# Fused causal attention and MLP on one core: scores issued three steps ahead of context, totals summed three steps behind, nine evenly spread TensorE sums a group

## The chip, the cores and the metric

One core of a Trainium2 chip (trn2) runs the whole program. The metric is device time in microseconds, the median of several executions. TensorE, VectorE, ScalarE, GpSimd and the DMA queue of SyncE are written PE, DVE, ACT, POOL and SP in the rows of the profile; SP issues all the transfers named here.

## The reference

A transformer layer over 4096 tokens of width 512: attention with 16 heads of 32, layer norm of the residual, a SiLU-gated MLP with int32 weights and per-row scales, and a second layer norm. The change is in the attention:

```python
scores = jnp.einsum('bshd,bthd->bhst', q / jnp.sqrt(jnp.float32(HEAD_DIM)), k)
causal = jnp.triu(jnp.ones((S, S), dtype=bool), 1)
scores = jnp.where(causal, NEG_INF, scores)
attn = jax.nn.softmax(scores, axis=-1)
ctx = jnp.einsum('bhst,bthd->bshd', attn, v)
```

## The kernel before

Three stages follow one another: `project` (queries, keys and values, with their norms, to DRAM), `attend` (the stage that is changed) and `finish` (output projection, MLP, norms). `finish` begins when `attend` has ended on every engine.

`attend` works on four groups of four heads (`NG`, `HG`). In a group the 4096 queries are cut into eight chunks of 512, `ch` 0 to 7, and the keys into 32 blocks of 128, `kb`. A step is one chunk with one key block; chunk `ch` has 4(ch+1) steps, because only keys up to the chunk's end count, and a group has 144 steps (`NS`). In each chunk the four blocks on the diagonal come at places 0, 2, 4 and 6 with full blocks between them (in chunk 0 at places 0 to 3). A diagonal block is computed on 512, 384, 256 or 128 columns of queries (`cut`) and its first 128 columns are masked.

For each step:

- `scores` on TensorE: two units, `p` = 0 and 1, of two heads each. A unit writes one of three PSUM buffers (`RING` = 3), so unit u waits until ScalarE has read unit u-3.
- ScalarE: one exponential a unit, from PSUM into one of six `probs` buffers in SBUF (`PB` = 6). Step t waits until step t-6 has been read by both TensorE and VectorE (`valued`, `added`).
- GpSimd masks a diagonal block in place (line 826), once both exponentials are done.
- VectorE adds the step's probabilities to `total` (lines 1011 and 1016), for the softmax denominators. Place 0 of a chunk shares one add with place 1.
- `weigh` on TensorE (line 881): values times probabilities for four heads, added up in `ctx_acc` over the chunk. It waits for the exponentials, the mask, and at place 0 for `ctx_taken`.

In ten steps of a group (`by_pe`) TensorE does the adding instead: eight more matmuls with a matrix of ones into `sums_acc` (line 889), and VectorE skips the step. When a chunk is done, `sum_total` (TensorE, line 900) adds `total` over the partitions, VectorE copies the result out (`take_sums`, line 997), ScalarE copies the context out (`take_ctx`, line 936), and SP stores both.

TensorE runs in program order, one iteration a step: the scores of step t+2 (`LAG` = 2), then the context of step t, then `sum_total` of a chunk whose last step was t-2. At the end of a group `sum_total` of chunk 7 follows the last step directly.

SP's order matters in two places. In group 0 the loads of keys and values 2 to 7 stand ahead of the stores of chunk 0 and the queries of chunk 3. In every later group this is the order:

```python
load("q", 0); load("kv", 0); load("q", 1)
for j in range(1, NCH):
    load("kv", j)
store(sp, before, NCH - 1)     # waits for take_sums, chunk 7 of the group before
for ch in range(2, NCH):       # queries of chunk 2 first
    load("q", ch); store(sp, g, ch - 2)
```

Of the kernel before, what the change touches and what calls it, by code (L numbers as in the profile page):

```python
# [38 lines left out]
P = 128  # L39
# [539 lines left out]
def attend(nc, io, dr, keep):  # L579

    LAG = 2
    T_LAG = LAG + 2
    PB = 6
    RING = 3

# [24 lines left out]

    def by_pe(t):

        ch, kb = steps[t]
        return not diagonal(t) and t - first[ch] >= ST * 2 and (t - first[ch]) % 10 == 0
# [9 lines left out]
    def masks_before(t):  # L624
        return sum(diagonal(x) for x in range(t))

    with ExitStack() as c:
# [202 lines left out]
        def _(pe):  # L830
# [21 lines left out]
            def scores(g, t):  # L852
                ch, kb = steps[t]
                if t in first:
                    mine = q_chunks[q_buffer[ch]]
                    pe.wait_ge(q_in[q_buffer[ch]], 64 * len(mine) * g + 64 * (mine.index(ch) + 1))
                if kb == ST * ch:
                    pe.wait_ge(k_in[ch], 48 * g + 64)
                for p in range(2):
                    u = 2 * t + p  # L860

                    pe.wait_ge(exped, 2 * NS * g + u + 1)
                    for i in range(2):
                        h = 2 * p + i
                        ins = pe.matmul(score[u % RING][:, i, cut(t):], keys[0:ROWS, kb // ST, h, kb % ST * P:(kb % ST + 1) * P],  # L865
                                        queries[0:ROWS, q_buffer[ch], h, cut(t):], start=True, stop=True)
                    ins.then_inc(scored, 1)
# [47 lines left out]
            for t in range(LAG):  # L915
                scores(0, t)
            for g in range(NG):
                group(g, g < NG - 1)

        @block.scalar  # L920
        def _(act):
# [39 lines left out]
        def _(dve):  # L961
# [37 lines left out]
            for g in range(NG):  # L999
                for t in range(NS):  # L1000
                    ch, kb = steps[t]
                    place = t - first[ch]
                    if not by_pe(t) and (place or not ch):
                        dve.wait_ge(exped, 2 * NS * g + 2 * t + 2 + RING)
                        if diagonal(t) or place == 1:
# [3 lines left out]
                        if place > 1:  # L1009
                            dve.wait_ge(added, NA * g + adds_before(t) + A_CREDIT)  # L1010
                            dve.tensor_tensor(into, into, now, ALU.add).then_inc(added, 1)  # L1011
                        elif place == 1:
# [551 lines left out]
```

## Time and profile before

| what | value |
| --- | --- |
| median of 3 runs | 2407.95 us (2407.69 to 2412.66) |
| profiled execution | 2409.09 us, span of the trace 2407.3 us |
| attend, from first score matmul to last sum | 334.7 to 1557.6 us |
| busy over the whole span | TensorE 2328.8 us (97%), VectorE 1774.3, ScalarE 1315.9, GpSimd 271.7 |
| mean granted TensorE clock | 0.987 |

A row of a timeline gives start, duration, engine, line, operation and tiles, how many instructions were merged, and in brackets how long the engine was idle before and what released it. A context step and a PE sum are eight matmul records each; score steps are four. The ends of matmuls are modelled and overlap the next start a little, so the cost of an iteration is read from the start of its scores to the start of the next iteration's scores.

### The profile page before, as it was taken

Reading aid. Unit: us, or ns where it says so; the run is one execution under the profiler, and the core shown is the slowest. Engines: PE = TensorE matmul, PEld = TensorE weight load, DVE = VectorE, ACT = ScalarE, POOL = GpSimd, SP = SyncE. Lnnn points to the kernel's source line nnn. Section 1 sums busy time; section 2 is a strip of 40 time slices with the busy share of each in tenths; the row PEclk is TensorE's granted clock in tenths of the full one; section 3 lists DMA queues with packets and bytes.
Section 4 is the critical chain, followed back from the end, with each engine's and each line's share of the span. In section 5 each row is a group of like instructions: output and inputs, shape, how many; then the busy total and the mean of one; then the engine's idle time right before and its main releaser. Section 6 shows DMA issues by size and latency. Waiting matters only on the chain. (4 is left out here: it accounts for less than half of the span.)

```text
span 2407.3 us, 34361 instructions
## 1 busy us (share of the span) xinstructions
PE 2328.8 (97%) x12546; PEld 1403.8 (58%) x12546; DVE 1774.3 (74%) x1826; ACT 1315.9 (55%) x1631; POOL 271.7 (11%) x269
## 2 busy tenths in 40 slices
PE   8999979999999999999999999869999999999997
PEld 7888843333343333434334343358888888888885
DVE  7777748889888898888988889845556565565554
ACT  4444458888888888888888888711111111111111
POOL 2111112201122010221102111000000000000000
PEclk9999989999999999999999999979999999999998
DMA  7777794101811008110081100091111021110100
GB/s 250 255 247 248 233 246 94 39 7 24 166 41 36 19 10 180 41 32 23 6 181 45 32 23 6 20 312 35 36 36 53 19 70 35 36 53 18 35 18 18
DMA packets 126868, 197.42 MB, mean 82 GB/s; under 512 B 15064, under 2 KB 40152, under 8 KB 126688
## 3 DMA queue, kind: packets, MB, share of 16 engines
q1 hardware_dynamic: 126704, 195.25, 28.9%
q8 instruction: 101, 1.65, 0.3%
q14 instruction: 63, 0.52, 0.1%
HBM read 122.83 MB, written 72.37 MB: 81 GB/s over the span
## 5 line engine op out<-in xcount | busy, mean ns | idle before, releaser
L947 ACT ACTIVATE probs<-score 128x1024 f32<-128x1024 f32 (+3 forms) x1152 | 1024.8, 957 | 180.1 <-PE score L865 157.4
L1011 DVE TENSOR_TENSOR total<-total,probs 128x2048 f32<-128x2048 f32 (+3 forms) x472 | 982.4, 2081 | 77.9 <-POOL probs L826 35.3
L865 PEld LDWEIGHTS score<-queries,keys 98*128 98x128 f32 x2304 | 375.9, 189 | 495.9 <-ACT probs L947 409.4
L865 PE MATMUL score<-queries,keys 98*128 98x512 f32 (+3 forms) x2304 | 655.0, 406 | 6.4 <-ACTq L931 6.1
L881 PE MATMUL ctx_acc<-probs,values 128*32 128x512 f32 (+3 forms) x3584 | 441.3, 564 | 9.3 <-POOL probs L826 9.2
L1350 ACT ACTIVATE hidden<-slot,gate_scale_sb 128x512 f32<-128x512 f32 x128 | 88.0, 688 | 625.2 <-PE slot L1279 625.2
L826 POOL TENSOR_SCALAR_AFFINE_SELECT probs<-probs 128x512 f32<-128x512 f32 x128 | 193.2, 1510 | 1006.9 <-ACT probs L947 1006.9
L1435 DVE SCALAR_TENSOR_TENSOR hidden<-slot,up_scale_sb,hidden 128x512 f32<-128x512 f32 x128 | 96.1, 751 | 265.3 <-ACT hidden L1350 265.3
L1279 PE MATMUL slot<-xt_hi,wg_sb 128*128 128x512 f32 x512 | 201.8, 394 | 5.2 <-issue 5.2
L1279 PE MATMUL slot<-xt_lo,wg_sb 128*128 128x512 f32 x512 | 200.2, 391 | 3.2 <-issue 3.2
L1290 PE MATMUL y<-wd_sb,h_hi 128*128 128x512 f32 x512 | 199.4, 389 | 1.4 <-DVE h_lo L1443 1.4
L1279 PE MATMUL slot<-xt_hi,wu_sb 128*128 128x512 f32 x512 | 199.7, 390 | 0.0
L1279 PE MATMUL slot<-xt_lo,wu_sb 128*128 128x512 f32 x512 | 199.6, 390 | 0.0
L1290 PE MATMUL y<-wd_sb,h_lo 128*128 128x512 f32 x512 | 199.2, 389 | 0.0
L344 PE MATMUL acc<-w_hi,x_hi 128*128 128x512 f32 x384 | 163.9, 427 | 7.2 <-DVE w_lo L495 7.2
L881 PEld LDWEIGHTS ctx_acc<-probs,values 128*32 128x32 f32 x3584 | 71.7, 107 | 157.2 <-issue 127.2
L344 PE MATMUL acc<-w_hi,x_lo 128*128 128x512 f32 x384 | 151.1, 394 | 0.0
L344 PE MATMUL acc<-w_lo,x_hi 128*128 128x512 f32 x384 | 150.6, 392 | 0.0
L881 PE MATMUL ctx_acc<-probs,first_values 128*32 128x512 f32 (+3 forms) x1024 | 132.8, 591 | 0.0
L1221 POOL TENSOR_TENSOR rstd<-veps,minus_half 128x1 f32<-128x1 f32 x64 | 36.7, 573 | 807.0 <-DVE veps L1399 807.0
L1016 DVE TENSOR_TENSOR total<-probs 128x2048 f32<-128x2048 f32 (+1 forms) x32 | 71.2, 2226 | 58.1 <-ACT probs L947 57.0
L1279 PEld LDWEIGHTS slot<-xt_hi,wg_sb 128*128 128x128 f32 x512 | 96.6, 189 | 29.2 <-issue 9.1
(103 smaller groups left out, 2088.7 us busy)
## 6 DMA issues: line engine op xcount, KB each, us to landing
keys<-k_hi SPq DMA_DIRECT2D x64, 256.0 KB
queries<-q_hi SPq DMA_DIRECT2D x64, 256.0 KB
wq_int<-in_wq SPq DMA_DIRECT2D x48, 256.0 KB, 3.3
wq_float<-wq_f SPq DMA_DIRECT2D x48, 256.0 KB, 2.8
x_raw<-in_x_t SPq DMA_DIRECT2D x32, 256.0 KB, 3.8
v_rows<-v_out SPq DMA_DIRECT2D x32, 256.0 KB, 2.3
q_hi<-part_hi SPq DMA_DIRECT2D x32, 256.0 KB, 2.5
q_lo<-part_lo SPq DMA_DIRECT2D x32, 256.0 KB, 2.8
```

What stands on the lines that cost most here:

```text
L344: ins = pe.matmul(bank[:], x[:, par, dc, rows], w[:, dc, m * D:(m + 1) * D], start=dc == 0 and a == 0, stop=dc == DC - 1 and a == 2)
L826: pool.affine_select(out=view, in_=view, compare_op=ALU.is_ge, fill=0.0, base=0, pattern=[[0, HG], [1, P]], channel_multiplier=-1).then_in ...
L865: ins = pe.matmul(score[u % RING][:, i, cut(t):], keys[0:ROWS, kb // ST, h, kb % ST * P:(kb % ST + 1) * P], queries[0:ROWS, q_buffer[ch], ...
L881: ins = pe.matmul(ctx[h * HD:(h + 1) * HD, n0:], value(kb)[:, h * HD:(h + 1) * HD], probs[:, t % PB, h, n0:], start=t in first, stop=t in ...
L947: act.activation(probs[:, t % PB, 2 * p:2 * p + 2, cut(t):], score[u % RING][:, :, cut(t):], ACT.Exp).then_inc(exped, 1)
L1011: dve.tensor_tensor(into, into, now, ALU.add).then_inc(added, 1)
L1016: dve.tensor_tensor(into, probs[:, (t - 1) % PB, :, cut(t):], now, ALU.add).then_inc(added, 2)
L1221: pool.tensor_tensor(rstd[:, k, st:st + 1], veps[:, k, st:st + 1], minus_half[:], ALU.pow).then_inc(rooted[k], 1)
L1279: ins = pe.matmul(slot[pos % 2][q][:], v(w[:, i, dc * P:(dc + 1) * P]), v(x[:, par, dc, :]), start=dc == 0 and a == 0, stop=dc == DC - 1 a ...
L1290: ins = pe.matmul(y[st][:], v(x[:, i % 2, st * P:(st + 1) * P]), v(wd[:, i, :]), start=i == 0 and a == 0, stop=i == IC - 1 and a == 1)
L1350: act.activation(hidden[:, i % 2, :], slot[pos % 2][0][:], ACT.Silu, scale=gate_scale[:, i:i + 1]).then_inc(gated, 1)
L1435: dve.scalar_tensor_tensor(hid, slot[pos % 2][1][:], up_scale[:, i:i + 1], hid, ALU.mult, ALU.mult)\
```

## The change

TensorE's iteration t now issues the scores of step t+3, and `sum_total` follows three steps behind the end of a chunk. For chunk 7 this goes over the group's border: it is issued behind context step 2 of the next group, and `take_sums` behind step 3 of VectorE. The scores are counted in units, and ScalarE's `take_ctx` moves to the first unit of the third step of the next chunk. The steps that TensorE sums are nine a group, spread evenly over the full steps from place 8 on: steps 32, 50, 59, 76, 94, 103, 120, 130 and 139, in place of 22, 34, 50, 70, 80, 94, 104, 122, 132 and 142. No instruction of a transfer is added or moved in SP's order.

```diff
-    LAG = 2
-    T_LAG = LAG + 2
+    LAG = 3
+    TOTAL_LAG = 3
     PB = 6
     RING = 3
+    PE_SUMS = 9
...
+    late = [t for t in range(NS) if not diagonal(t) and place(t) >= 2 * ST]
+    pe_sums = {late[(2 * i + 1) * len(late) // (2 * PE_SUMS)] for i in range(PE_SUMS)}
+
     def by_pe(t):
 
-        ch, kb = steps[t]
-        return not diagonal(t) and t - first[ch] >= ST * 2 and (t - first[ch]) % 10 == 0
+        return t in pe_sums
...
+    scored_before = [2 * (t + LAG) + 2 for t in range(NS)]
+    taken_behind = {scored_before[last[ch]] - 2: ch for ch in range(NCH)}
...
-            def group(g, after):
-
+            def group(g, before, after):
+
+                done = early
                 for t in range(NS):
-                    if t + LAG < NS:
-                        scores(g, t + LAG)
-                    elif after:
-                        scores(g + 1, t + LAG - NS)
+                    for u in range(done, scored_before[t]):
+                        if u < 2 * NS:
+                            scores(g, u)
+                        elif after:
+                            scores(g + 1, u - 2 * NS)
+                    done = scored_before[t]
                     weigh(g, t)
-                    if t + LAG - T_LAG in last:
-                        sum_total(g, last.index(t + LAG - T_LAG))
-                sum_total(g, NCH - 1)
-
-            for t in range(LAG):
-                scores(0, t)
+                    if t - TOTAL_LAG in last:
+                        sum_total(g, last.index(t - TOTAL_LAG))
+                    elif before is not None and t == TOTAL_LAG - 1:
+                        sum_total(before, NCH - 1)
...
-                        if p == 0 and t - LAG in last:
-                            take_ctx(g, last.index(t - LAG))
-                        elif p == 0 and t == LAG - 1 and before is not None:
+                        if u in taken_behind:
+                            take_ctx(g, taken_behind[u])
+                        elif u + 2 * NS in taken_behind and before is not None:
                             take_ctx(before, NCH - 1)
...
-                    if t - T_LAG - 1 in last:
-                        take_sums(g, last.index(t - T_LAG - 1))
-                take_sums(g, NCH - 1)
+                    if t - TOTAL_LAG - 1 in last:
+                        take_sums(g, last.index(t - TOTAL_LAG - 1))
+                    elif g and t == TOTAL_LAG:
+                        take_sums(g - 1, NCH - 1)
+            take_sums(NG - 1, NCH - 1)
```

TensorE at the start of chunk 5 in group 0, before: the first row with 384 columns is the score of the chunk's place 2, and the row behind it the context of place 0.

```order
1978 L865 MATMUL score<-queries,keys 128x384 x4
1979 L881 MATMUL ctx_acc<-probs,values 32x512 x4
1980 L865 MATMUL score<-queries,keys 128x512 x4
1981 L881 MATMUL ctx_acc<-probs,first_values 32x512 x4
1982 L900 MATMUL sums_acc<-total,ones 32x512 x4
1983 L865 MATMUL score<-queries,keys 128x256 x4
1984 L881 MATMUL ctx_acc<-probs,values 32x384 x4
1985 L865 MATMUL score<-queries,keys 128x512 x4
1986 L881 MATMUL ctx_acc<-probs,first_values 32x512 x4
1987 L865 MATMUL score<-queries,keys 128x128 x4
1988 L881 MATMUL ctx_acc<-probs,values 32x256 x4
```

The same place after the change, from the score of place 2 on:

```order
1976 L874 MATMUL score<-queries,keys 128x384 x4
1977 L890 MATMUL ctx_acc<-probs,values 32x512 x4
1978 L898 MATMUL sums_acc<-probs,ones 32x512 x4
1979 L874 MATMUL score<-queries,keys 128x512 x4
1980 L890 MATMUL ctx_acc<-probs,values 32x512 x4
1981 L874 MATMUL score<-queries,keys 128x256 x4
1982 L890 MATMUL ctx_acc<-probs,first_values 32x512 x4
1983 L874 MATMUL score<-queries,keys 128x512 x4
1984 L890 MATMUL ctx_acc<-probs,values 32x384 x4
1985 L909 MATMUL sums_acc<-total,ones 32x512 x4
1986 L874 MATMUL score<-queries,keys 128x128 x4
```

Behind the score of place 2 there now stands the context of chunk 4's last step with a PE sum, and the context of place 0 comes only behind the score of place 3; each masked context step (512, 384 and 256 columns at places 0, 2 and 4) has one more score step ahead of it.

TensorE at the border of groups 0 and 1, before: `L900` is the total of chunk 7, and the scores of 384, 256 and 128 columns are steps 1, 2 and 3 of the new group.

```order
2154 L865 MATMUL score<-queries,keys 128x384 x4
2155 L881 MATMUL ctx_acc<-probs,values 32x512 x4
2156 L900 MATMUL sums_acc<-total,ones 32x512 x4
2157 L865 MATMUL score<-queries,keys 128x256 x4
2158 L881 MATMUL ctx_acc<-probs,first_values 32x512 x4
2159 L865 MATMUL score<-queries,keys 128x128 x4
2160 L881 MATMUL ctx_acc<-probs,first_values 32x384 x4
2161 L865 MATMUL score<-queries,keys 128x512 x4
2162 L881 MATMUL ctx_acc<-probs,first_values 32x256 x4
2163 L865 MATMUL score<-queries,keys 128x512 x4
```

The same place after the change:

```order
2154 L874 MATMUL score<-queries,keys 128x256 x4
2155 L890 MATMUL ctx_acc<-probs,values 32x512 x4
2156 L874 MATMUL score<-queries,keys 128x128 x4
2157 L890 MATMUL ctx_acc<-probs,first_values 32x512 x4
2158 L874 MATMUL score<-queries,keys 128x512 x4
2159 L890 MATMUL ctx_acc<-probs,first_values 32x384 x4
2160 L874 MATMUL score<-queries,keys 128x512 x4
2161 L890 MATMUL ctx_acc<-probs,first_values 32x256 x4
2162 L909 MATMUL sums_acc<-total,ones 32x512 x4
2163 L874 MATMUL score<-queries,keys 128x384 x4
```

The total of chunk 7 moved from directly behind the group's last context step to behind the context of step 2, past the scores of steps 3, 4 and 5 and three context steps. VectorE's copy of that sum (`sums_out<-sums_acc`) moved with it, from ahead of the adds of the new group to behind the first four of them:

```order
1625 L1034 COPY total<-probs 128x4x128
1626 L1030 TENSOR_TENSOR total<-probs 128x4x384
1627 L1025 TENSOR_TENSOR total<-total,probs 128x4x256
1628 L1025 TENSOR_TENSOR total<-total,probs 128x4x128
1629 L1012 COPY sums_out<-sums_acc 128x512
1630 L1030 TENSOR_TENSOR total<-probs 128x2048
```

## Rows read from the trace of the kernel before

**Rows 1.** Window of attend: busy PE, PEld, DVE, ACT, POOL; clock, DMA share, GB/s

```profile
334.70:1557.60 1222.90, 1212.87 (x7488) 486.42 (x7488) 1073.22 (x543) 1040.13 (x1184) 193.20 (x128) 1.00 0.25 54
```

**Rows 2.** Waits in attend: engine, line, released by: total us, times, longest

```profile
PE ctx_acc L881 <- POOL probs L826: 9.2, 28, 0.5
```

**Rows 3.** Timeline, steady steps of chunk 7, group 1

```profile
899.89 14.27 DVE L1011 TENSOR_TENSOR total<-total,probs 128x2048 f32<-128x2048 f32 x6
...
907.65 1.19 PE L865 MATMUL score<-queries,keys 98*128 98x512 f32 x4
908.50 1.94 ACT L947 ACTIVATE probs<-score 128x1024 f32<-128x1024 f32 x2 [0.18 <-PE score L865]
...
909.77 1.19 PE L865 MATMUL score<-queries,keys 98*128 98x512 f32 x4
```

**Rows 4.** Timeline, score steps around one PE sum

```profile
900.41 1.19 PE L865 MATMUL score<-queries,keys 98*128 98x512 f32 x4
...
903.39 1.20 PE L865 MATMUL score<-queries,keys 98*128 98x512 f32 x4
```

**Rows 5.** Timeline of TensorE, place 0 of chunk 4, group 1

```profile
726.87 0.97 PE L865 MATMUL score<-queries,keys 98*128 98x384 f32 x4
...
728.76 1.25 PE L865 MATMUL score<-queries,keys 98*128 98x512 f32 x4
```

**Rows 6.** Timeline, place 0 of chunk 5, group 1

```profile
767.53 2.29 DVE L1011 TENSOR_TENSOR total<-total,probs 128x2048 f32<-128x2048 f32 x1
767.60 2.71 POOL L826 TENSOR_SCALAR_AFFINE_SELECT probs<-probs 128x512 f32<-128x512 f32 x1 [29.66 <-ACT probs L947]
...
768.93 0.97 PE L865 MATMUL score<-queries,keys 98*128 98x384 f32 x4
769.07 0.60 ACT L936 ACTIVATE ctx_out<-ctx_acc 128x512 f32<-128x512 f32 x1 [0.39 <-PE ctx_acc L881]
...
770.42 1.06 PE L881 MATMUL ctx_acc<-probs,values 128*32 128x512 f32 x8 [0.52 <-POOL probs L826]
771.41 0.19 PEld L865 LDWEIGHTS score<-queries,keys 98*128 98x128 f32 x1 [0.84 <-ACT probs L947]
```

**Rows 7.** Timeline of TensorE, place 4 of chunk 4, group 1

```profile
735.37 0.66 PE L865 MATMUL score<-queries,keys 98*128 98x128 f32 x4
736.27 0.64 PE L881 MATMUL ctx_acc<-probs,values 128*32 128x256 f32 x8 [0.25 <-POOL probs L826]
736.84 0.50 PE L865 MATMUL score<-queries,keys 98*128 98x512 f32 x1
```

**Rows 8.** Timeline of TensorE, place 4 of chunk 2, group 1

```profile
677.03 0.66 PE L865 MATMUL score<-queries,keys 98*128 98x128 f32 x4
...
678.20 1.20 PE L865 MATMUL score<-queries,keys 98*128 98x512 f32 x4
```

**Rows 9.** The masks' line: least, median and most ns of one

```profile
L826 POOL TENSOR_SCALAR_AFFINE_SELECT probs<-probs x128: 630/1338/2736, 338.1 to 1499.5; 128x512 f32<-128x512 f32 x128
```

**Rows 10.** Timeline of TensorE, first score of chunk 3, group 0

```profile
382.19 1.06 PE L881 MATMUL ctx_acc<-probs,values 128*32 128x512 f32 x8
...
383.55 1.19 PE L865 MATMUL score<-queries,keys 98*128 98x512 f32 x4 [0.30 <-DMA queries<-shift]
```

**Rows 11.** Timeline of TensorE behind the border of groups 1 and 2

```profile
955.03 1.19 PE L865 MATMUL score<-queries,keys 98*128 98x512 f32 x4
...
968.91 1.19 PE L865 MATMUL score<-queries,keys 98*128 98x512 f32 x4
```

**Rows 12.** Timeline of SP there: stores of chunks 7 and 0

```profile
952.08 0.50 SPq L693 DMA_DIRECT2D sums<-sums_out  x1
...
968.05 0.50 SPq L693 DMA_DIRECT2D sums<-sums_out  x1
```

**Rows 13.** Windows there, columns as in the first group

```profile
961.00:963.00 2.00, 2.00 (x20) 0.69 (x12) 1.59 (x1) 1.35 (x3) 0.32 (x1) 1.00 0.07 18
...
975.00:977.00 2.00, 2.00 (x17) 0.95 (x17) 1.55 (x1) 1.74 (x3) 1.30 (x1) 1.00 0.01 3
```

More of the change, by code:

```diff
@@ L609, in diagonal, with place @@
         return steps[t][1] >= ST * steps[t][0]
+    def place(t):
+        return t - first[steps[t][0]]
+    late = [t for t in range(NS) if not diagonal(t) and place(t) >= 2 * ST]
+    pe_sums = {late[(2 * i + 1) * len(late) // (2 * PE_SUMS)] for i in range(PE_SUMS)}
     def by_pe(t):
-        ch, kb = steps[t]
-        return not diagonal(t) and t - first[ch] >= ST * 2 and (t - first[ch]) % 10 == 0
+        return t in pe_sums
     adds = [t for t in range(NS) if not by_pe(t)]
@@ L850, in _, with scores @@
             pe.sem_inc(totaled, 2)
-            def scores(g, t):
+            def scores(g, u):
+                t, p = divmod(u, 2)
                 ch, kb = steps[t]
-                if t in first:
+                if p == 0 and t in first:
                     mine = q_chunks[q_buffer[ch]]
                     pe.wait_ge(q_in[q_buffer[ch]], 64 * len(mine) * g + 64 * (mine.index(ch) + 1))
-                if kb == ST * ch:
+                if p == 0 and kb == ST * ch:
                     pe.wait_ge(k_in[ch], 48 * g + 64)
[L859 to L867, printed above, removed]
+                pe.wait_ge(exped, 2 * NS * g + u + 1)
+                for i in range(2):
+                    h = 2 * p + i
+                    ins = pe.matmul(score[u % RING][:, i, cut(t):], keys[0:ROWS, kb // ST, h, kb % ST * P:(kb % ST + 1) * P],
+                                    queries[0:ROWS, q_buffer[ch], h, cut(t):], start=True, stop=True)
+                ins.then_inc(scored, 1)
             def weigh(g, t):
@@ L901, in sum_total @@
                 ins.then_inc(totaled, 1)
-            def group(g, after):
+            def group(g, before, after):
+                done = early
                 for t in range(NS):
-                    if t + LAG < NS:
-                        scores(g, t + LAG)
-                    elif after:
-                        scores(g + 1, t + LAG - NS)
-                    weigh(g, t)
-                    if t + LAG - T_LAG in last:
-                        sum_total(g, last.index(t + LAG - T_LAG))
-                sum_total(g, NCH - 1)
-            for t in range(LAG):
-                scores(0, t)
+                    for u in range(done, scored_before[t]):
[4 more added lines that the diff above has]
+                    done = scored_before[t]
+                    weigh(g, t)
+                    if t - TOTAL_LAG in last:
+                        sum_total(g, last.index(t - TOTAL_LAG))
+                    elif before is not None and t == TOTAL_LAG - 1:
+                        sum_total(before, NCH - 1)
+            early = scored_before[NS - 1] - 2 * NS
+            for u in range(early):
+                scores(0, u)
             for g in range(NG):
-                group(g, g < NG - 1)
+                group(g, g - 1 if g else None, g < NG - 1)
+            sum_total(NG - 1, NCH - 1)
         @block.scalar
@@ L1001, in _ @@
                     ch, kb = steps[t]
-                    place = t - first[ch]
-                    if not by_pe(t) and (place or not ch):
+                    if not by_pe(t) and (place(t) or not ch):
                         dve.wait_ge(exped, 2 * NS * g + 2 * t + 2 + RING)
-                        if diagonal(t) or place == 1:
+                        if diagonal(t) or place(t) == 1:
                             dve.wait_ge(masked, NM * g + masks_before(t + 1))
```

4 lines of the change are left out of this document (2 added, 2 removed).

## The prediction

> **What bounds the kernel now.** I read the page's busy times first, then the window of attend alone, then the waits in it, then timelines. Attend takes 1222.9 us of the span, and TensorE is busy for 1212.9 of them at the full granted clock; VectorE is busy for 1073.2 and ScalarE for 1040.1 [rows 1]. So TensorE sets the stage's length with 10.0 us of gaps, and VectorE has 150 us to spare over the stage. The biggest gaps with a releaser are 28 waits of context steps for GpSimd's mask, 9.2 us in all, 0.5 the longest [rows 2]. A steady step shows why nothing else matters much: scores start at 907.65 and again at 909.77, 2.12 us a step, while ScalarE's two exponentials take 1.94 and then wait 0.18 for the next score [rows 3]. ScalarE runs right behind the scores. A long wait that the profile books on the exponentials for weight loads is no cost here, since the matmuls around it leave no gap.
>
> The depth of the look-ahead does not pace such a step. What ties scores to exponentials is the ring of three units, and that distance is the same with two or three steps ahead. What the look-ahead sets is how long an exponential and its mask have before TensorE wants them.
>
> **PE sums.** One iteration with a PE sum goes from 900.41 to 903.39, 2.98 us, against 2.12 without [rows 3, 4]: 0.86 us for a sum. One less in each of four groups gives 4 x 0.86 = 3.4 us. VectorE gets four more adds. Six adds in a row take 14.27 us, so 2.4 us each with its gap [rows 3]: 9.6 us more on an engine with 150 to spare. Locally it falls back 2.4 - 2.12 = 0.28 us a step until a PE sum or a chunk's place 0 lets it catch up. The last of those six adds starts at 899.89 + 14.27 - 2.29 = 911.87, while the exponentials of its step ended at 908.50 + 1.94 = 910.44: 1.4 us behind. A buffer is wanted again by the exponential six steps on, which starts five steps and a gap later, 5 x 2.12 + 0.18 = 10.8 us. An add that starts less than 10.8 - 2.3 = 8.5 us late costs nothing. One step that is no longer skipped adds 2.4, and the longest new stretch without a sum (chunk 5, 16 places) some 6 x 0.28 = 1.7 more. I cost the adds at nothing; the cover that hides them is this buffer slack.
>
> **Mask waits.** At place 0 of chunk 4, with no wait, an iteration takes 728.76 - 726.87 = 1.89 us [rows 5]; at place 0 of chunk 5 it takes 771.41 - 768.93 = 2.48 [rows 6]: 0.59 lost. At place 4 of chunk 4 it is 736.84 - 735.37 = 1.47, against 678.20 - 677.03 = 1.17 where nothing waits [rows 7, 8]: 0.30 lost. Of the 28 waits, 8 are of the first kind (chunks 2 and 5 of each group), 20 of the second. After the change each masked context step has one more score and context step ahead of it, at least some 1.2 us (the cheapest iteration, rows 8, is the bound from below), against at most 0.59 lost. So all should go, unless masks get later. Two of the 28, one of each kind, lie ahead of a load in group 0 and are taken out below. That leaves 7 x 0.59 + 19 x 0.30 = 9.8 us.
>
> How late can a mask be? The mask at place 0 of chunk 5 starts at 767.60, 0.07 us behind an add of 2.29 us, and takes 2.71 [rows 6]; the median is 1.34 and the most 2.74 [rows 9]. So it seems to stand still while the add runs. The Trainium skill (SBUF — State Buffer, SBUF: two separate sides) has a rule for that: a VectorE operation with two SBUF inputs and a GpSimd operation exclude one another for the whole instruction. By that rule more adds on VectorE mean more masks at the long end. If all masks took the 2.74 us of the longest, place 4's would come 2.74 - 1.34 = 1.4 us later than the median one, against the 1.2 to 2.1 us gained; I expect at most a few tenths to survive at some places, and the sum takes nothing for it.
>
> **Context taken.** At place 0 the context step also waits for ScalarE's copy of the last chunk's context, 769.07 to 769.67 in chunk 5 [rows 6]. Its place relative to the last context step is kept, and a full score step of 1.19 us instead of 0.97 now lies in between. No cost. The copy delays the exponentials behind it. The tightest spot that follows is the second score unit of place 4, which needs the first exponential of place 3: the copy ends 0.74 us after the next scores began (769.67 - 768.93), two exponentials of about 0.7 and 1.0 follow, so 2.4 us, and TensorE gets there after 2.12 + 0.35 = 2.5. Bounds: nothing, or up to 0.1 x 28 = 3 us. I take nothing, since the same race stands in the rows of before, one place earlier.
>
> **A load in group 0.** Chunk 3's first scores start at 383.55 on a DMA of queries [rows 10]. That load stands behind SP's loads of keys and values and does not hang on TensorE. TensorE would now reach these scores a context step sooner, and sooner by the waits removed before, and must wait for the same load. Everything won earlier in group 0 is lost there, and the context step that used to run ahead of this score, started at 382.19 and worth 1.06 us with a little overlap, now runs behind it: +1.0 us. The same holds for the longer fill at the start of attend, which costs nothing extra for that reason.
>
> **Queries of chunk 2 at the borders.** SP stores chunk 7's sum, then loads these queries. The store was issued at 952.08, and the transfers were nearly over in 961 to 963 [rows 12, 13]. The sum now comes after score step 5 and context step 2, which end in before at about 955.03 + 1.19 = 956.2; add 0.9 for VectorE's copy: the store goes out at 957.1, 5 us later. The next such store with its query load, issued at 968.05, has its traffic over in 975 to 977 [rows 12, 13], so 7 to 8 us from store to landing: 964.5 to 966 here. The scores of step 12 start at 968.91 [rows 11], after the change one context step and one mask wait sooner, 967.6. Slack 1.6 to 3 us where it was 6; no cost.
>
> **Tail.** After the last scores TensorE had two context steps, a PE sum and the last context step; now it has four context steps, much the same time, and the last add starts no later. 0.
>
> Sum: -3.4 - 9.8 + 1.0 = -12.2 us. The profiled execution would go from 2409.1 to 2396.9; it lies 1.1 above the median of the runs, 2407.95, so the median becomes 2395.75, and I say 2395.5.
>
> **Rivals.**
> - The mask waits only move: the next scores wait for their exponentials instead, and the gain is -3.4 + 1.0, or 2405.5 us. For it: ScalarE runs without a gap around places 1 to 3. Against it: it is idle 0.18 us in each steady step, and the price of the waits shows in start-to-start times. Chance 0.07.
> - VectorE falls six buffers behind in chunks 5 to 7: then each of its four extra adds comes onto the path, +9.6 in place of nothing, 2405 us. It needs adds 8.5 us late where I see 1.4 plus at most 4. Chance 0.03.
> - Slower: the queries of chunk 2 come late at three borders. Each us beyond the slack costs 3 us. It cancels the gain when they land 12.2 / 3 = 4.1 us beyond TensorE's arrival, so 6 to 7 us later than I reckon; at 6 us beyond, the time is 2395.5 + 18 = 2413.5. Nothing in the rows is that slow. Chance 0.03. A mild form, 1 to 2 us beyond, gives 2398.5 to 2401.5: chance 0.07.
> - My forecast: 0.80.
>
> **How the numbers follow.** A change of 0.2% is 4.8 us, about what this kernel's measurement can tell. Low end: small waits that I left out go too (attend's gaps are 10.0 us in all by modelled ends, but a wait of 0.25 by gap is 0.30 by starts, so up to 12 with the lesser ones), some 2 to 3 us more, and a run-to-run spread of 2: 2390.5. High end: the ring's 3 us and the mild load case: 2401. Faster is my case plus the mild load case, 0.87; same takes the first two rivals, 0.09; slower 0.04.
>
> **What would show it.** Right: no wait of context steps for masks; PE idle in attend near 3 us; the iteration at place 0 of chunk 5 without a gap; steady steps still 2.12; VectorE idle one or two us behind the fourth add of a group, waiting for the sum; the scores of chunk 3 in group 0 waiting about 2 us for queries. Wrong: a gap before the scores of step 12 in groups 1 to 3, ScalarE waiting for adds, or steady steps longer than 2.12.

## The result, and the profile after

| | median | runs | profiled |
| --- | --- | --- | --- |
| before | 2409.23 us | 4 (2407.69 to 2412.66) | 2409.09, span 2407.3 |
| after | 2391.01 us | 4 (2389.47 to 2391.17) | 2389.47, span 2387.7 |

The ratio is 0.9921, 95% interval 0.9904 to 0.9938. The change takes away 18.2 us by the medians and 19.6 by the two spans, where 12.2 were forecast. The direction held, and the size was half as much again as the sum said. The range, 2390.5 to 2401, was counted from a median of 2407.95 us. As a time, 2391.01 lies just inside it. But the ratio measured here, applied to 2407.95, gives 2388.9, and that is below the low end. One execution each of after_pad64, before_pad64 and six_placed in the experiments below took 3125 to 4510 us and is left out of their ratios.

I cut both spans at the first score matmul and at the end of attend's last sum. By spans the 19.6 us are 1.3 ahead of attend (334.7 to 333.4), 14.4 in attend (1222.8 to 1208.5) and 3.9 behind it (849.8 to 845.8).

The window of attend after, columns as in [rows 1]:

```profile
333.40:1541.90 1208.50, 1207.44 (x7456) 488.29 (x7456) 1094.79 (x547) 1038.86 (x1184) 166.16 (x128) 1.00 0.25 54
```

TensorE's gaps fell from 10.0 us to 1.1, and it does 32 matmuls less: four sums of eight. VectorE does four adds more, of 2.29 us, and is busy 21.6 us longer. Most of the rest are 41 adds that begin while a mask runs and take 2.5 to 2.8 us in place of 2.29, 10.7 us in all; before there was none such. The waits of attend's TensorE work after, columns as in [rows 2]:

```profile
PEld score L874 <- DMA queries<-shift: 0.8, 1, 0.8
...
PE ctx_acc L890 <- ACT ctx_out L951: 0.6, 3, 0.2
...
PE sums_acc L909 <- DVE total L1025: 0.4, 1, 0.4
```

The 28 waits for masks are gone. In their place stand three of 0.2 us for ScalarE's copy of the context, at the group borders. The start of chunk 5 in group 1, TensorE, VectorE, ScalarE and GpSimd, to be held against [rows 6]:

```profile
763.45 1.20 PE L874 MATMUL score<-queries,keys 98*128 98x512 f32 x4
764.58 1.07 PE L890 MATMUL ctx_acc<-probs,values 128*32 128x512 f32 x8
765.57 0.79 PE L874 MATMUL score<-queries,keys 98*128 98x256 f32 x4
766.29 1.07 PE L890 MATMUL ctx_acc<-probs,first_values 128*32 128x512 f32 x8
767.28 1.20 PE L874 MATMUL score<-queries,keys 98*128 98x512 f32 x4
...
752.16 7.08 DVE L1025 TENSOR_TENSOR total<-total,probs 128x2048 f32<-128x2048 f32 x3
761.45 2.29 DVE L1030 TENSOR_TENSOR total<-probs 128x2048 f32<-128x2048 f32 x1 [2.21 <-ACT probs L962]
...
763.59 0.60 ACT L951 ACTIVATE ctx_out<-ctx_acc 128x512 f32<-128x512 f32 x1 [1.34 <-PE sums_acc L898]
...
759.37 0.63 POOL L836 TENSOR_SCALAR_AFFINE_SELECT probs<-probs 128x512 f32<-128x512 f32 x1 [29.45 <-ACT probs L962]
```

The context of place 0 starts at 764.58; its mask had ended at 759.37 + 0.63 = 760.00, where before it ended 0.1 us ahead of the context step. The mask also takes 0.63 us in place of 2.71. It begins 0.13 us behind VectorE's last add (752.16 + 7.08 = 759.24), and VectorE then stands idle for 2.21 us, because one of the nine TensorE sums (step 59) is now chunk 4's last step. The iteration runs from 763.45 to 765.57, 2.12 us, with no gap. All masks of the program, columns as in [rows 9]:

```profile
L836 POOL TENSOR_SCALAR_AFFINE_SELECT probs<-probs x128: 630/1110/2791, 336.8 to 1483.3; 128x512 f32<-128x512 f32 x128
```

The median fell from 1338 ns to 1110 though VectorE adds more. The longest still takes 2791. Before, 119 of the 128 masks begin while an add runs, and after 95 do (median 1.34 and 1.36 us); the others, 9 and 33, take 0.63 to 0.64 us, all but one. So a mask is long where it begins beside an add, as the rule of the Trainium skill (SBUF — State Buffer, SBUF: two separate sides) that the prediction quotes has it; by that rule, where the adds lie counts, and not their number.

In group 0 the predicted wait for chunk 3's queries did not come. TensorE after, the score at 380.59 being the first of chunk 3. Its queries had landed 0.17 us earlier:

```profile
379.59 1.07 PE L890 MATMUL ctx_acc<-probs,values 128*32 128x512 f32 x8
380.59 1.21 PE L874 MATMUL score<-queries,keys 98*128 98x512 f32 x4
381.73 1.06 PE L890 MATMUL ctx_acc<-probs,values 128*32 128x512 f32 x8
```

Behind attend there is a place that the prediction did not look at. The first matmuls of the MLP's gate in `finish`, before:

```profile
1598.14 0.77 PE L1279 MATMUL slot<-xt_hi,wg_sb 128*128 128x512 f32 x1 [5.23 <-issue]
...
1599.98 0.63 PE L1279 MATMUL slot<-xt_hi,wg_sb 128*128 128x512 f32 x1
1603.77 0.59 PE L1279 MATMUL slot<-xt_lo,wg_sb 128*128 128x512 f32 x1 [3.16 <-issue]
```

And after:

```profile
1583.35 0.76 PE L1295 MATMUL slot<-xt_hi,wg_sb 128*128 128x512 f32 x1 [5.24 <-issue]
...
1585.19 0.63 PE L1295 MATMUL slot<-xt_hi,wg_sb 128*128 128x512 f32 x1
1585.62 0.63 PE L1295 MATMUL slot<-xt_lo,wg_sb 128*128 128x512 f32 x1
```

In both kernels TensorE waits 5.2 us ahead of this block. Before, TensorE stops again after five matmuls, for 3.16 us, and no semaphore releases it ("issue"); after, it runs through. That is 3.2 of the 3.9 us behind attend, in code that the change does not touch.

### The profile page after: what moved, and what is told of

Its sections match the earlier page's. It is cut to its first block and busy times, and to the rows that moved or that the text cites. A ratio compares the mean times of both kernels' runs of the same rounds, so it can differ in the third digit from the quotient of the medians.

```text
span 2387.7 us, 34309 instructions
## 1 busy us (share of the span) xinstructions
PE 2321.6 (97%) x12514; PEld 1404.7 (59%) x12514; DVE 1795.6 (75%) x1830; ACT 1314.7 (55%) x1631; POOL 244.7 (10%) x269
## 5 line engine op out<-in xcount | busy, mean ns | idle before, releaser
L1025 DVE TENSOR_TENSOR total<-total,probs 128x2048 f32<-128x2048 f32 (+3 forms) x476 | 1004.3, 2110 | 72.1 <-POOL probs L836 20.1
L836 POOL TENSOR_SCALAR_AFFINE_SELECT probs<-probs 128x512 f32<-128x512 f32 x128 | 166.2, 1300 | 1017.3 <-ACT probs L962 1017.3
L1306 PEld LDWEIGHTS y<-wd_sb,h_hi 128*128 128x128 f32 x512 | 96.1, 188 | 22.1 <-DVE h_lo L1459 2.2
```

The costliest lines, as they stand in the source:

```text
L836: pool.affine_select(out=view, in_=view, compare_op=ALU.is_ge, fill=0.0, base=0, pattern=[[0, HG], [1, P]], channel_multiplier=-1).then_in ...
L1306: ins = pe.matmul(y[st][:], v(x[:, i % 2, st * P:(st + 1) * P]), v(wd[:, i, :]), start=i == 0 and a == 0, stop=i == IC - 1 and a == 1)
```

## The experiments

Three questions were open: how much of attend's gain is the look-ahead's and how much the sums'; why attend gave 14.4 us for 12.2; and whether the 3.2 us behind attend are luck, a matter of time, or one of the program's length. Times in us; "stop" is TensorE's second wait in the first gate block; the ratio is to the kernel before on the same chip, whose median there stands last.

| kernel | median | ratio, 95% | attend | behind it | stop | before |
| --- | --- | --- | --- | --- | --- | --- |
| e1_lag3_alone | 2400.97 | 0.9953 (0.9938 to 0.9968) | 1213.3 | 849.9 | 3.18 | 2411.87 |
| e2_nine_sums_alone | 2403.02 | 0.9963 (0.9950 to 0.9975) | 1221.9 | 847.7 | none | 2411.87 |
| e3_lag_back_to_2 | 2403.21 | 0.9962 (0.9949 to 0.9975) | 1221.7 | 846.0 | none | 2411.87 |
| e4_ten_sums_as_before | 2398.78 | 0.9945 (0.9933 to 0.9957) | 1211.9 | 850.9 | 3.22 | 2411.87 |
| before_again | 2412.61 | 1.0001 (0.9992 to 1.0010) | 1223.0 | 853.5 | 3.34 | 2412.64 |
| after_again | 2393.88 | 0.9930 (0.9919 to 0.9942) | 1209.0 | 847.2 | none | 2412.64 |
| lag4 | 2396.99 | 0.9939 (0.9926 to 0.9952) | 1213.6 | 847.2 | none | 2412.64 |
| sums5 | 2393.24 | 0.9920 (0.9907 to 0.9933) | 1213.4 | 847.8 | none | 2412.64 |
| after_pad64 | 2392.25 | 0.9913 (0.9892 to 0.9934) | 1209.0 | 846.7 | none | 2411.81 |
| before_pad64 | 2413.26 | 0.9999 (0.9987 to 1.0011) | 1226.5 | 852.6 | 3.32 | 2411.81 |
| before_pad192 | 2413.31 | 1.0002 (0.9993 to 1.0012) | 1222.2 | 851.8 | 3.31 | 2411.81 |
| six_placed | 2390.81 | 0.9904 (0.9890 to 0.9919) | 1202.5 | 850.5 | 4.94 | 2411.81 |
| after_mm16 | 2399.46 | 0.9950 (0.9935 to 0.9965) | 1208.6 | 853.9 | 4.20 | 2411.79 |
| before_mm48 | 2409.77 | 0.9994 (0.9984 to 1.0003) | 1225.3 | 847.9 | none | 2411.79 |
| six_late | 2392.66 | 0.9919 (0.9906 to 0.9933) | 1210.1 | 846.8 | none | 2411.79 |
| seven_late | 2386.06 | 0.9896 (0.9881 to 0.9911) | 1201.4 | 846.7 | none | 2411.79 |

### The change taken apart

The kernel before with the look-ahead alone, and with the new sums alone:

```diff
-    LAG = 2
+    LAG = 3
```

```diff
-        ch, kb = steps[t]
-        return not diagonal(t) and t - first[ch] >= ST * 2 and (t - first[ch]) % 10 == 0
+        return t in {32, 50, 59, 76, 94, 103, 120, 130, 139}
```

> Only the look-ahead goes from 2 to 3 steps; ten TensorE sums and the places of the totals stay. Theory A (the look-ahead removes the waits for masks and for the context copy, 11 us in attend, and what changed outside attend is chance): attend falls from 1222.8 to about 1211.9 us, the mask waits of the context steps are gone, and time outside attend is anywhere between 1179 and 1185 us. Theory B (the change also shortens the stage behind attend by 4 us, whichever part of it does that): if the look-ahead does it, the time outside attend is near 1179 as in the changed kernel, and the whole falls by 16 us. Theory C (the waits went because totals and sums moved, not the look-ahead): attend stays within 3 us of 1222.8.

> Only the set of steps that TensorE sums is that of the change, nine a group; look-ahead 2 and totals as before. Theory A: attend falls by 4 x 0.86 = 3.4 us to about 1219.4, with all mask waits still there (28, some 9 us); outside attend chance. Theory C: the evenly spread sums give the mask waits more room and attend falls by clearly more than 3.4. Theory B (nine sums shorten the stage behind): outside attend near 1179.

The changed kernel with its look-ahead put back to 2, and with the old ten sums (`return t in {22, 34, 50, 70, 80, 94, 104, 122, 132, 142}`):

```diff
-    LAG = 3
+    LAG = 2
```

> The changed kernel with the look-ahead put back to 2 steps, the nine sums and the later totals kept. Theory A: attend returns to about 1219 us (1208.5 + 11), with the mask waits back. Theory C: it stays near 1208.5. If the later totals cost or give something of their own, attend differs from that of the kernel with nine sums alone by that much; I expect under 1 us.

> The changed kernel with the ten summed steps of before. Theory A: attend 1208.5 + 3.4 = 1211.9 us. A rival for the sums (their even spread matters beyond their number): attend rises by more than 5 us.

e1 shows no wait for a mask. So the deeper look-ahead alone takes them all away. It does pay for the load of group 0, which the whole change did not. TensorE in e1:

```profile
385.49 1.20 PE L865 MATMUL score<-queries,keys 98*128 98x512 f32 x4 [1.80 <-DMA queries<-shift]
```

e2 keeps some of the mask waits, but not all. Its wait and that of e3:

```profile
PE ctx_acc L880 <- POOL probs L825: 5.3, 16, 0.5
```

```profile
PE ctx_acc L890 <- POOL probs L836: 3.7, 7, 0.8
...
PE ctx_acc L890 <- ACT probs L962: 3.1, 5, 0.7
```

Moving the sums takes 12 of the 28 named waits away by itself, but little of their time. Behind the first 22 us of attend, the iterations with a masked context step at places 0 and 4 lose 11.8 us before and 9.5 in e2, by their starts: 2.3 us is all that the new places give alone. With the look-ahead alone attend is 9.5 us shorter, 11.0 without the 1.5 us by which its load wait is longer than the 0.3 of before. So nearly all of this gain is the look-ahead's. Against e4, the change has four sums less and is 3.4 us shorter in attend, 2.8 without e4's load wait of 0.6; against e1 it is 4.8 shorter, 3.0 without the load wait. Four sums were costed at 3.4.

e2 and e3 gained hardly anything in attend, 0.9 and 1.1 us, and the reason is its opening. Ten us that begin 10 us into attend, in e2 and in before:

```profile
344.50:354.50 10.00, 10.00 (x39) 4.47 (x38) 3.46 (x3) 6.35 (x8) 1.97 (x2) 0.50 1.11 199
```

```profile
344.70:354.70 10.00, 10.00 (x70) 4.14 (x68) 5.50 (x4) 8.76 (x12) 2.63 (x3) 1.00 1.13 188
```

TensorE runs at a granted clock of 0.50, its lower level of 1.2 GHz, and gets through 39 matmuls in place of 70. The spell of lower clock in which attend begins lasts 27.3 us in e2 and 17.1 in before, and e2 reaches the first scores of chunk 3 at 52.5 us of attend where before has them at 48.8: 3.7 us lost. Both also wait 1.5 us for VectorE's last add ahead of the last sum, 1.1 more than before. For e2, -3.4 for the sums, -2.3, +3.7 and +1.1 make the 0.9 that it gained. All four agree on the stop behind attend: it is there with ten sums (e1, e4) and not with nine (e2, e3), whatever the look-ahead.

### The same two again, one step more, and fewer sums

Both kernels unchanged, then two numbers of the changed one:

```diff
-    LAG = 3
+    LAG = 4
```

```diff
-    PE_SUMS = 9
+    PE_SUMS = 5
```

> The kernel before once more, unchanged, against itself. Theory A (time outside attend is chance, it follows how long the clock is granted at half at the two borders of attend): attend near 1222.8 us (up to 4 more where the opening spell of half clock is the longer one), outside attend anywhere in 1179 to 1187, ratio to itself 1.000. Theory B (the change itself shortens the rest): outside attend 1184 or more here, and 1180 or less in the repeated changed kernel.

> The changed kernel once more. Theory A: attend 1208.5 us within 1, plus a wait of up to 2 us at the first scores of chunk 3 in group 0 if the queries land later than 47.2 us after the start of attend; outside attend 1179 to 1187; the ratio to before then nearer to (1222.8 - 1208.5) / 2408, that is 0.994, than the 0.992 first measured. Theory B: ratio 0.992 again and outside attend 1180 or less.

> The changed kernel with the scores four steps ahead. The mask waits are gone already with three, so theory A gives nothing more in groups 1 to 3; in group 0 TensorE reaches the first scores of chunk 3 one context step (1.0 us) sooner and waits 1 to 3 us for the queries, and the opening fill is longer. Attend 1209.5 to 1211. If look-ahead depth itself paced the steps, attend would fall below 1207.

> The changed kernel with five TensorE sums a group in place of nine. If a sum costs TensorE 0.86 us and VectorE has room, attend falls by 16 x 0.86 = 13.8 us to 1194.7, and the whole to about 2379 to 2383. Rival: VectorE, with 2.4 us more for each add, falls six buffers behind in the long chunks and ScalarE waits for it; then attend gains less than 10 us and ScalarE shows waits for adds.

On another chip the change is worth 18.7 us. The stop repeats: 3.34 and none. The load does not: after_again waits 0.98 us for chunk 3's queries, which landed 47.0 us after attend's start in the profile of after and 46.2 to 50.7 in the others that load them at the same place.

A fourth step of look-ahead costs 3.1 us by the medians, with intervals that overlap, and 4.6 in attend by the two profiles. There is no mask wait left to take away. The iteration with the scores of place 4 (256 columns) and a full context step now takes 1.88 us, where it takes 1.71 in after and 1.66 undisturbed; all of this kind together lose 4.8 us more than in after. ScalarE's copy of the context stands there: in chunk 5 of group 1 it starts at 767.93, 0.14 us behind the start of these scores, and the next exponential comes behind it. VectorE waits for sums as well, since they are issued deeper behind the work, but nothing shows that this reaches TensorE:

```profile
DVE sums_out L1012 <- PE sums_acc L909: 39.7, 25, 3.6
```

With five sums a group, 16 x 0.86 = 13.8 us of TensorE work go, and the median moves by 0.6. Attend is even longer in the profile, which is of the slowest of the five executions: 1213.4 us, where 1194.7 was expected. Two fences show the end of its TensorE timeline and ScalarE's wait for buffers:

```profile
1534.58 3.64 PE L890 MATMUL ctx_acc<-probs,values 128*32 128x512 f32 x32
1546.94 1.93 PE L909 MATMUL sums_acc<-total,ones 128*32 128x512 f32 x8 [8.72 <-DVE total L1025]
```

```profile
ACT probs L962 <- DVE total L1025: 16.8, 24, 3.5
```

VectorE is 8.7 us late at the very end, where nothing hides it, 8.3 more than in after, and its lateness reaches ScalarE's buffers 24 times. TensorE feels that only about the three borders, 4.6 us in all (at 952.57 its scores wait 0.79 us for ScalarE, which at 951.71 had waited 0.93 for an add). Another 4.9 us lie at the load of group 0: TensorE waited 3.3 us for it, and a spell of lower clock of 3.4 us followed that wait. The three make 17.8 of the 18.7 us. This is the cover that the prediction named for the adds, and here is where it ends.

### Is the stop a matter of the program's length?

The rival was that the stop depends on when `finish` begins. The theory, D in the expectations, put it on instructions: they come by transfers of 16384 bytes on a queue of their own, one about every 21 us of attend. In attend of before TensorE does a median of 256 records between two of them, which makes 64 bytes an instruction. By the theory the transfer is one of 256 instructions, and the one wanted in the gate block is late if it is asked for when the weight loads fill the DMA engines. The DMA view of before in the stop:

```profile
q1 hardware_dynamic: 795, 1.45, 103.6%
q8 instruction: 1, 0.02, 1.9%
```

The 16 engines are full, and the one instruction packet is among 795 others. Where the stop falls should then go by the number of TensorE's instructions ahead of it. A sum is 16 records (eight matmuls, eight weight loads), so the four sums less are 64 records less. First I added no-operations at TensorE's start (64 to after; 64 and 192 to before):

```diff
+            for _ in range(64):
+                pe.nop(nofuse=True)
             pe.wait_ge(ones_ready, 1)
```

> The changed kernel with 64 no-operations on TensorE ahead of its first score, where it waits anyway. A summed step is 16 TensorE instructions in the trace, so 64 is what the four dropped sums took out of the program. Theory D (3.2 us of the gain lie behind attend: with ten sums the program has an instruction fetch that TensorE must wait for in the fifth matmul pair of the first gate block, and dropping 64 instructions moved that place): the wait of 3.2 us inside line 1279's group of before comes back here, in the same place, and the time behind attend goes from 846 or 847 to 849 to 851 us; attend stays 1208.5 to 1209.5. Rival B (nine sums or the end of attend itself shortens what follows): no such wait, 846 to 848.

> The kernel before with the same 64 no-operations. Theory D: the wait of 3.2 us behind the fifth matmul of the first gate block moves to another place, 32 matmuls earlier, or shrinks where TensorE waits for something else anyway; attend 1222.8. Rival B: the wait stays exactly where it is.

> The kernel before with 192 no-operations, which is 64 short of 256. If the places where fetches stop TensorE repeat every 256 instructions or a divisor of it, this program lies as the changed kernel does: theory D then has the wait of 3.2 us gone and the time behind attend 846 to 848 us with ten sums and two steps ahead. Rival B: 849 to 853 as in both profiles of before.

They changed nothing: not the stop, and not the times at which instruction packets went in attend (10.7 to 10.9 us ahead of its end in all three kernels of before, 6.2 to 6.3 in both of after). So they did not shift the stream, and tested nothing. Matmuls do shift it. Each of these, of 32 columns, is four records (two matmuls, two weight loads), so 16 make up for four sums, and 48 put 192 records more into before, which is 64 short of one whole transfer:

```diff
             pe.wait_ge(ones_ready, 1)
+            for _ in range(16):
+                pe.matmul(sums[0:HD, 0:HD], ones[:], ones[:], start=True, stop=True)
```

> The changed kernel with 16 small matmuls of the ones matrix (32 columns) ahead of the first score, in the wait there; they are 64 TensorE instructions in the trace, as many as the four dropped sums. The no-operations of the earlier try left the times of the instruction transfers as they were, so they took no room in the program; these do. Theory D: the instruction transfer that lay 6.2 us ahead of attend's end goes back to about 10.9 us ahead of it, and the wait of 3.2 us in the first gate block returns; time behind attend 849 to 851 us, attend 1208.5 to 1210. Rival E (the wait hangs on what attend computes, not on where its instructions lie): no wait, 846 to 848.

> The kernel before with 48 such matmuls, 192 instructions, 64 short of 256; the transfers of 16384 bytes hold 256 instructions of 64 bytes. Theory D: its fetches lie as in the changed kernel (one some 6 us ahead of attend's end), the wait of 3.2 us is gone and the time behind attend is 846 to 848 us, with ten sums and two steps ahead. Rival E: wait as before, 849 to 853. Attend 1222.8, or up to 4 more with a long opening at half clock.

The gate block of after with 16 matmuls, and of before with 48:

```profile
1588.50 0.63 PE L1297 MATMUL slot<-xt_hi,wg_sb 128*128 128x512 f32 x1
1593.33 0.59 PE L1297 MATMUL slot<-xt_lo,wg_sb 128*128 128x512 f32 x1 [4.20 <-issue]
```

```profile
1606.91 0.63 PE L1281 MATMUL slot<-xt_lo,wg_sb 128*128 128x512 f32 x1
1607.34 0.63 PE L1281 MATMUL slot<-xt_hi,wg_sb 128*128 128x512 f32 x1
1607.76 0.63 PE L1281 MATMUL slot<-xt_lo,wg_sb 128*128 128x512 f32 x1
```

The stop comes back with nine sums, and goes with ten. The last packet in attend moved as well: 10.5 us ahead of attend's end in after_mm16, 5.4 in before_mm48. That settles it against time: before_mm48 reaches the block later than before does, after_mm16 earlier, and the stop follows the count. after_mm16 lies 8.5 us above after, on another chip; 4.2 of them are the stop, and the wait ahead of the block is 1.5 longer in its profile. By the medians before_mm48 was 2.0 below the kernel before on its chip, which is not clear of noise (0.9984 to 1.0003). That it lost the stop is read from its profile, which also has a load wait of 2.9 us. That the full DMA engines make the packet late is what the rows suggest; no run emptied them, and the packet itself takes 1.1 us there and 1.0 where they are nearly idle.

### Fewer sums, put where VectorE catches up

sums5 failed at the end and not in the middle, so the sums went behind, and the queries of chunk 3 were loaded in group 0 right behind its keys 3, which takes the load wait out:

```diff
-        return t in pe_sums
+        return t in {50, 76, 103, 120, 131, 142}
...
+                        if j == 3:
+                            load("q", 3)
...
-                    if before is not None or ch > 2:
+                    if before is not None or ch > 3:
```

> The changed kernel with six TensorE sums a group, steps 50, 76, 103, 120, 131 and 142, so that VectorE is never far behind at the end of a group, and with the queries of chunk 3 in group 0 loaded behind keys and values 3. Three sums fewer in each group give 12 x 0.86 = 10.3 us if VectorE keeps up: attend 1198.2, the whole about 2380 to 2384. With five evenly spread sums TensorE waited 8.7 us for the last add; here that wait should be near 0.4 as in the changed kernel. No wait for the queries of chunk 3. Rival: VectorE is nearly full, ScalarE waits for adds, and attend stays above 1203.

Attend fell to 1202.5 us, with 4.5 of them a wait for the last add. But the stop is back, 4.94 us, after the first matmul:

```profile
1585.20 0.59 PE L1297 MATMUL slot<-xt_lo,wg_sb 128*128 128x512 f32 x1 [4.94 <-issue]
```

Six sums are 16 less than ten over four groups, 16 x 16 = 256 records: exactly one transfer, so the stream lies nearly as it does with ten. The same kernel with later sums, `{76, 98, 120, 128, 135, 142}` and `{55, 76, 98, 120, 128, 135, 142}`:

> As the kernel with six placed sums, with four of the six in chunk 7: steps 76, 98, 120, 128, 135 and 142. VectorE is then less behind at the group's end: the wait of TensorE for the last add falls from 4.5 us to 1 or less, attend 1198 to 1200 us. By theory D it lies in the program as six placed sums do, with a wait of 3 to 5 us in the first gate block; the whole 2384 to 2388.

> Seven sums: as six late ones, with step 55 added. Attend 4 x 0.86 = 3.4 us above six late ones, 1201.5 to 1203.5. Its program is 128 instructions shorter than the changed kernel's: if the wait in the first gate block is gone there (theory D allows either), the whole is as fast as with six, 2383 to 2387.

six_late missed. It has no early sum to let VectorE catch up:

```profile
ACT probs L964 <- DVE total L1027: 44.5, 82, 1.6
```

It has six sums as well and yet no stop. That sent me back to the traces, to count all of TensorE's records ahead of the gate block's first matmul: weight loads twice (a load and its matmul, since some matmul records are missing), semaphore records once, and 123 others that are the same in every program.

| kernels | loads | semaphores | all, modulo 256 | stops after | there, modulo 256 |
| --- | --- | --- | --- | --- | --- |
| before, its pads, e1, e4 | 9027 | 290 | 35 | matmul 5 | 45 |
| after_mm16 | 9027 | 294 | 39 | matmul 3 | 45 |
| six_placed | 8899 | 298 | 43 | matmul 1 | 45 |
| six_late | 8899 | 302 | 47 | none | |
| seven_late | 8931 | 298 | 107 | none | |
| before_mm48 | 9123 | 290 | 227 | none | |
| after, its repeat and pad, e2, e3, lag4 | 8995 | 294 | 231 | none | |
| sums5 | 8867 | 298 | 235 | none | |

Every stop lies at the same place of the stream, 45 behind a multiple of 256, in eight profiles of seven programs. six_late waits on four semaphores more than six_placed, so this place lies one matmul ahead of the block, in the 5.2 us that TensorE waits there anyway. This count was made from the traces after the runs; that the place is where one transfer's instructions end is my reading of it.

The place alone does not make a stop. In the kernels with 227 to 235 in the table TensorE passes it 9.5 to 11.6 us behind the block's first matmul, with the DMA engines as full (104 to 106%), and runs through. What the traces have in common is time: in all 18, a packet of 16384 bytes starts 3.2 to 3.4 us behind the block's first matmul, and all eight stops end 5.6 to 5.8 us behind it, wherever they began. So the stop is as long as TensorE is early. At five matmuls in it lasts 3.2 to 3.3 us, at three 4.2, at one 4.9. This fits the reading that TensorE waits for what that packet brings.

seven_late has the lowest median of all, 0.9896 of before (0.9881 to 0.9911), 25.7 us, where the change alone has 0.9921 and 0.9930. Its interval overlaps that of six_placed, so only its lead over the repeated change is clear of noise:

```profile
335.50:1536.90 1201.40, 1199.82 (x7392) 485.76 (x7392) 1120.43 (x555) 1039.13 (x1184) 163.70 (x128) 1.00 0.25 55
```

```profile
1535.80 1.07 PE L911 MATMUL sums_acc<-total,ones 128*32 128x512 f32 x8 [0.89 <-DVE total L1027]
```

Eight sums less than the change has are 6.9 us at 0.86; attend is 7.1 shorter, and VectorE is 0.9 us late at the end.

## Why the prediction was wrong: the mechanism held, the sum did not

The step that failed is the sum of -12.2 us. It was made for attend alone and put everything outside attend at nothing, without giving a reason. The spans show 5.3 us there: 3.2 are the stop in `finish`, 0.7 the rest behind attend, 1.3 ahead of it. Inside attend two terms were mis-sized: the mask waits, forecast at 9.8 and measured at 11.0, and the load of group 0, forecast at +1.0 and measured at nothing in this profile. Attend gave 14.4 us for 12.2.

**What bounds the kernel.** Right. TensorE is still busy for all but 1.1 us of attend, and steady steps are 2.12 us in both traces.

**PE sums.** Right at -3.4: 2.8 to 3.0 by e4 and e1, and 7.1 for eight sums less in seven_late. That the adds cost nothing was right too: the last sum waits 0.4 us for VectorE. But the cover is thinner than its 150 us of spare time says: six well-placed sums and sums5 ran out of it at the end of attend, which the prediction's figure of 8.5 us of slack in the buffers does not describe, since there is no later step at the end.

**Mask waits.** The mechanism was right and the term was too small. I took the time of every iteration above what iterations with the same pieces of work take where nothing delays them. The sum is 18.2 us before and about 7 after, by which trace the undisturbed time is taken from. That is some 11 less, and attend's 14.4 less the four sums' 3.4 is 11.0. In before, about 12.3 of the 18.2 are at masked context steps and copies of the context. I had counted 28 waits with a name and priced the rest at nothing; chunk 1's place 0 loses 0.26 us in each group as well, where the context step needs ScalarE's copy. Below the range's low end I had named "small waits that I left out", 2 to 3 us: these are it.

**Masks later.** The fear of later masks did not come true, since the masks got shorter, 1300 ns on average for 1510.

**Context taken.** I took nothing, with 3 as the bound. The scores of place 4 now take a median of 1.71 us where 1.66 is usual: 1.85 us in all with the rest of that kind, and 0.6 at the borders. So this race is real, as lag4 shows with 4.8 us more of it, and it is the 2.4 us that attend did not give back of the 12.3 and more.

**The load in group 0.** The +1.0 was not paid in the profile of after, where TensorE was ready at 47.19 us behind attend's start and the queries had landed at 47.02. It is 0.7 to 1.0 in after_pad64 and after_again, 0.6 and 1.8 in e4 and e1, 3.3 in sums5, and nothing in after_mm16. What failed here is "must wait for the same load": the load does not hang on TensorE, as I said, but it is not at a fixed time either.

**Borders.** Right. The store of chunk 7's sum, the load behind it, and the time at which the scores of step 12 start in group 2 (959.14):

```profile
948.86 0.50 SPq L703 DMA_DIRECT2D sums<-sums_out  x1
...
951.43 0.30 SPq L92 DMA_DIRECT2D queries<-shift  x1
```

The last of these loads is issued 7.7 us ahead of the scores, and no TensorE wait is named there. In groups 1 to 3 the queries landed 2.5 to 2.8 us ahead of these scores, where it was 6.2 to 6.8 before; 1.6 to 3 was forecast. VectorE waits 2.02 us for that sum, as forecast. In sums5, where VectorE is late with the copy, the queries land 0.04 to 0.07 us ahead of the scores: there the slack is used up.

**Outside attend.** The sum was made for attend alone, and nothing was said of `finish`. 3.2 us of the gain lie there, the stop. mm16 and mm48 show that it goes by the number of instructions ahead and not by what attend does; that the change moved it out of the way was luck. The 1.3 us ahead of attend are chance: e1, with the same program there, began attend at 336.6.

Of the rivals, none came. The waits that did move are the 2.4 us above.

Account by spans: 12.2 forecast, +1.0 for the load, +1.2 for waits left out, less those that came, +3.2 for the stop, +0.7 for the rest behind attend, +1.3 ahead of it, 19.6.

## What to carry to other kernels

Price a wait by the start-to-start time of iterations with the same work, and do it for all iterations, not just for those with a named releaser. Work moved to an engine with spare time is free only as long as that engine has steps left in which to catch up, so put the last relief close to the end. When a change alters the number of TensorE's instructions, look for "issue" waits in stages behind it that have full DMA queues, and repeat the comparison with the count restored before you credit the change with them.

## What was unexpected of the hardware

- TensorE can stop in the middle of a matmul sequence for 3.2 to 4.9 us, with no semaphore in it, where the DMA engines are 104% booked. It stops at one place of its instruction stream modulo 256, and goes on 5.6 to 5.8 us behind the block's first matmul. Adding 16 small matmuls in `attend`'s opening brought the stop back, and adding 48 took it away. 64 no-operations did neither, and added no record.
- The landing time of one load, issued on the same queue at the same place of the program, differed by 4.5 us between the 15 profiles that have it there (46.2 to 50.7 us behind attend's start).
- In three of seven profiles with a look-ahead of 2 the spell of lower clock in which attend begins lasted 27.3 us; in the eleven with 3 or 4 steps it was 20.5 at most. In e2 TensorE was busy for all ten us shown above and the granted clock stayed at 0.50. Why is open: the three share neither the sums nor the rest of the program, and no experiment was aimed at it.
